# The common expert's up projection by pairs of tiles from the fifth tile on, with the ranks in another PSUM bank

## The chip, the cores and the metric

The kernel runs on one core of one Trainium2 chip. The metric is the device time of one execution in microseconds (us). All data are float32.

## What is computed

A vision block of one layer. 64 images of 3x96x96 are cut into 16x16 patches: 36 tokens an image, 2304 tokens of width 192. The steps are: a patch projection plus a position row; `h = h + attention(layernorm(h))` with 12 heads of 16; and `h = h + ffn(layernorm(h))`, where the FFN is a mixture of 9 experts, each 192 to 768 to 192 with an exact Gelu:

```
route_prob = softmax(xt @ Ws + bs);  p = max(route_prob);  routes = argmax(route_prob)
h = gelu(einsum('td,edf->tef', xt, W1) + b1, approximate=False)
out = einsum('tef,efd->ted', h, W2) + b2
common = out[:, 0, :];  sel = the row of out that routes picks
final = where(routes == 0, common * scaling, pe * sel + (1 - pe) * common)
```

Expert 0 (the common expert) is computed for every token, and the expert that the router picks for each token besides.

## The kernel before

**Tiles and steps.** The 2304 tokens are 18 tiles of 128. Everything up to the routing is one software pipeline, written out step by step: every engine runs its own `main_step(s, ...)` for s = 0 to 38, and an operation with lag L works in step s on tile s - L. On TensorE the lags that matter here are: projection of the attention output 10 (`project_o`), transpose of the normalised FFN input 11 (`transpose_xn2`), router 12 (`route`), up projection of the common expert 20 (`common_up` and `ffn_up_rest`), its down projection 21 (`common_down`). So tile 4 goes up in step 24 and down in step 25. The attention proper ends in step 23, `project_o` ends in step 27, `transpose_xn2` in step 28 and `route` in step 29. From step 30 on TensorE has only up and down projections.

**Order on TensorE within a step** of 24 or later: up projection, (in step 30: `count_ranks`), `route`, `common_down`, `transpose_xn2`, `project_o`.

**The up projection of one tile** is six chunks of 128 hidden columns. A chunk is a matmul of the 128x128 weights with a moving operand of 128 columns (L623, contraction over features 0 to 127) and a matmul with contraction over the last 64 features (L631). Chunks 0 to 2 of L631 use rows 0 to 63 of the array, chunks 3 to 5 rows 64 to 127, and the two kinds alternate. Chunks 0 to 2 lie in bank 6, 3 to 5 in bank 7. ScalarE applies Gelu with its bias chunk by chunk (L855). The down projection is six matmuls of 192 columns (L641) into bank 0 for even tiles and bank 2 for odd ones. In the trace a float32 matmul of these shapes shows as two records, so "x12" is six matmuls.

**What orders the steps.** All engines run their instructions in program order, with semaphores between them.
- `common_down(n)` for an even n waits until the router's sums of tile n + 10 are added (`log_copied`), since both use bank 0. For an odd n it doesn't.
- VectorE does in each step: `norm_xn2` (L915; it waits for GpSimd's `rstd_h2`, L1306 and L1308, of the step before), then `add_log` (L1043), then `add_common` (L1047), then `add_attention` (L1031, with L1034 and L1037), which waits for `project_o`.
- `project_o` in an odd step waits until `add_common` has emptied bank 0.
- `route(t)` waits for the saved transpose of tile t, which ScalarE copies (`copy_xn2`, L793 to L795) after its Gelus of the step before.
- `count_ranks` in step 30 (two matmuls of 162 columns, L703 and L704) counts, for each token, the earlier tokens of its expert. VectorE makes slots from it (`slots`, from L1153). GpSimd then scatters the 18 tiles of normalised rows by slot into a packed buffer in DRAM with 18 indirect DMAs (L1357). The sync engine waits for all 18 (`scattered`), loads the first two groups of 128 packed rows (L466), issues a load of slot rows and four stores of output rows (L467, L456), and goes on with the third group (L475).

**The second phase** is 25 groups of 128 packed rows, each with its own expert: transpose (L514, L515), copy by ScalarE, up (L623, L631), Gelu (L855), down (L641), scaled and added to the output. `W1R` holds the up weights of two groups.

**Memory.** One SBUF region, `ARENA`, holds first the patches and projection weights and later the hidden rows `HT`, the gathered rows and the routing scratch `RT`.

Of the kernel before, what the change touches and what calls it, by code (L numbers as in the profile page):

```python
# [22 lines left out]
ACT = mybir.ActivationFunctionType  # L23
AX = mybir.AxisListType

P = 128
# [4 lines left out]
TOKENS = IMAGES * SEQ  # L31
# [16 lines left out]
WCOLS = DFF + FH  # L48
EXPERTS = 9
EPS = 1e-5  # L50


GROUPS = (TOKENS + (EXPERTS - 1) * (P - 1)) // P
# [39 lines left out]
def vit_kernel(nc, patches, conv_w, conv_b, pos, w_qkv, w_o, gq, gk, w_router, w1, w1_rest, w2, b2, consts, ids, out):  # L93
# [4 lines left out]
    with ExitStack() as ctx:  # L98
# [36 lines left out]
            return CST[0:rows, a:b]  # L135


        ARENA = sb("ARENA", 5800)
        marks = [0]

        def cut(n):
            a = marks[0]
            marks[0] += n
            assert marks[0] <= 5800
            return ARENA[:, a:a + n]

        PT = [cut(KC * P) for _ in range(2)]
# [4 lines left out]
        QKN = [cut(4 * P) for _ in range(2)]  # L152
        VST = [cut(D) for _ in range(2)]
        marks[0] = 0
        HT = [cut(DFF) for _ in range(2)]
        XF = [cut(ROW) for _ in range(2)]
        YR = [cut(D) for _ in range(2)]
        BASE = [cut(D) for _ in range(4)]
# [52 lines left out]
        def xn2t(t):  # L211

            at = (2 + t % 2) * TOKENS + t // 2 * 2 * P
            return QK[:, at:at + 2 * P]

        def single(p):

# [272 lines left out]
        def _(pe):  # L490
# [154 lines left out]
            def common_down(n):  # L645
                if n >= 2:
                    pe.wait_ge(y_used, n - 1)
                if n % 2:
                    pe.wait_ge(qk_normed, TILES)
                else:  # L650
                    pe.wait_ge(log_copied, min(n + UP_START - MIXER_START, TILES))
                ffn_down(n, n % 2, 0)

            def route(t):
                s = t + 2 + MIXER_START
# [29 lines left out]
            def common_up(t):  # L685
# [3 lines left out]
                pe.wait_ge(xn2t_saved, t + 1)  # L689
                ffn_up_first(t, xn2t(t), W1, t >= 1)  # L690

            def turn_b1():
                pe.wait_ge(b1_in, 16)
                pe.wait_ge(h2_added, TILES - MIXER_START)
                pe.transpose(bank[0][:, 0:EXPERTS * FC], B1[0:EXPERTS * FC, :],
                             ident[0:EXPERTS * FC, 0:EXPERTS * FC]).then_inc(b1_turned, 1)

            def count_ranks():

                pe.wait_ge(chosen, 1)  # L700
                onehot = RT[:, 0:TE]
                pe.wait_ge(s_shifted, STEPS)
                pe.matmul(bank[4][:, 0:TE], const("before"), onehot, start=True, stop=True)  # L703
                pe.matmul(bank[5][:, 0:TE], const("ones"), onehot, start=True, stop=True).then_inc(ranks_done, 1)  # L704

            def main_step(s, ks):
                kc, kq, kp, kx, k_scores, k_weigh, kw, k1, kr, kf, kh = ks
                if s == TILES:
                    turn_b1()
                if kc is not None:  # L710
                    conv(kc, 0, KC // 2)
                if kf is not None:
                    common_up(kf)
                if k_scores is not None:
                    scores(k_scores, 0, k_scores)
                if kc is not None:
                    conv(kc, KC // 2, KC)
                if kf is not None:
                    ffn_up_rest(kf, xn2t(kf), W1)
                if s == MIXER_START + TILES + 2:  # L720
                    count_ranks()
                if kq is not None:
                    transpose_qk(0, kq)
                if k_weigh is not None:
                    weigh_v(k_weigh, 0)
                if kp is not None:
                    project_qk(kp)
                if kr is not None:
                    route(kr)
                if kh is not None:  # L730
                    common_down(kh)
                if k_scores is not None:
                    scores(k_scores, 1, k_scores)
                if k1 is not None:
                    transpose_xn2(k1)
                if kp is not None:
                    project_v(kp)
                if kw is not None:
                    project_o(0, kw)
                if kx is not None:  # L740
                    transpose_xn(0, kx)
                if k_weigh is not None:
                    weigh_v(k_weigh, 1)
# [34 lines left out]
        def _(act):  # L778
# [68 lines left out]
            def gelu(n, par, b1, guard):  # L847
                for g in range(2):
# [7 lines left out]
                                              bias=b1[:, bias:bias + 1])  # L856
                    last.then_inc(gelu_done, 1)

            def main_step(s, ks):
                kx, kv, kq, k_exp, k_o, ko, k1, kg = ks  # L860
                if s == TILES:
# [8 lines left out]
                    copy_qkT(kq)  # L870
                if k_exp is not None:
                    exp_scores(k_exp, 0, k_exp)
                if kg is not None:
                    gelu(kg, kg % 2, B1T, kg >= 2)
                if k_o is not None:
                    copy_o(k_o, 0)
                if k1 is not None:
# [34 lines left out]
        def _(dve):  # L912
# [237 lines left out]
            def slots():  # L1150

                dve.wait_ge(ranks_done, 1)
                then(dve.tensor_copy(by_expert(counts), bank[5][:, 0:TE].rearrange("p (t e) -> p e t", e=EXPERTS)))  # L1153
                then(dve.tensor_tensor_scan(running, const("keep"), counts, 0.0, ALU.mult, ALU.add))
                then(dve.tensor_tensor(before, running, counts, ALU.subtract))

# [5 lines left out]
                then(dve.tensor_tensor(per_e(2), per_e(1), per_e(0), ALU.subtract))  # L1162
                then(dve.tensor_scalar(per_e(3), per_e(2), float(P), None, ALU.mult))
                then(dve.tensor_tensor(by_expert(before), by_expert(before), per_e(3).unsqueeze(2).to_broadcast([P, EXPERTS, TILES]), ALU.add))
                then(dve.tensor_tensor(by_tile(scratch), bank[4][:, 0:TE].rearrange("p (t e) -> p t e", e=EXPERTS),
                                       before.rearrange("p (e t) -> p t e", t=TILES), ALU.add))
                then(dve.tensor_tensor(scratch, scratch, onehot, ALU.mult))
                then(dve.reduce_sum(top, by_tile(scratch), axis=AX.X))
# [284 lines left out]
```

## Time and profile before

| | |
|---|---|
| median of 3 runs | 388.1 us (388.03 to 388.18) |
| the profiled execution's own time | 386.88 us |
| its span | 385.0 us |
| TensorE busy | 364.3 us, 95% |
| VectorE, ScalarE, GpSimd busy | 172.2, 163.9, 188.3 us |
| granted TensorE clock, mean | 0.993 |

TensorE is busy nearly all of the span, and no other engine is half busy. The shares are means over phases that differ: the steps with attention, the steps without it, and the 25 groups. The views that count are those of single steps and of the passage to the groups. The profiled execution is 1.2 us below the median of the timed runs.

### The profile page before, as it was taken

To read this page: it belongs to the slowest core of one execution; us is meant where nothing else is said; L and a number is where in the kernel's file an instruction comes from. 1 tells how busy PE (TensorE), PEld (TensorE's weight loads), DVE (VectorE), ACT (ScalarE), POOL (GpSimd) and SP (SyncE) were. 2 spreads that over 40 slices of the span, in tenths; PEclk is the share of its full clock that TensorE was granted. 3 is DMA by queue.
4 is the path that set the end of the run, shared out by engine and by line. 5 is a ranking of instruction groups with operands and counts; after the bars stand their busy time and mean duration, and the time that the engine had idled before them with its cause. 6 is when DMAs were issued, how large, how long until landed. Compare 5 with 4: busy or idle time off the path is not lost. (4 is left out here: it accounts for less than half of the span.)

```text
span 385.0 us, 10445 instructions
## 1 busy us (share of the span) xinstructions
PE 364.3 (95%) x3291; PEld 325.6 (85%) x3292; DVE 172.2 (45%) x595; ACT 163.9 (43%) x553; POOL 188.3 (49%) x307
## 2 busy tenths in 40 slices
PE   6799999999999999899999999998999999999991
PEld 5677877788888888788888899997999999999991
DVE  3365767777777787544232265411112211111111
ACT  0122233333333354778444454335545544555540
POOL 1657977777777787443013006740333333444333
PEclk9999999999999999999999999999999999999997
DMA  7764335353321435435000905626666776676630
GB/s 243 234 207 120 101 105 162 94 156 91 90 79 48 130 113 166 124 97 187 20 0 14 245 2 142 217 80 147 150 170 160 176 187 164 167 165 164 155 76 0
DMA packets 40589, 49.58 MB, mean 129 GB/s; under 512 B 10412, under 2 KB 32313, under 8 KB 40553
## 3 DMA queue, kind: packets, MB, share of 16 engines
q1 hardware_dynamic: 34641, 42.95, 37.8%
q0 software_dynamic: 5024, 5.72, 8.8%
q10 hardware_dynamic: 888, 0.45, 0.4%
q8 instruction: 21, 0.34, 0.4%
q14 instruction: 15, 0.12, 0.1%
HBM read 39.84 MB, written 10.27 MB: 130 GB/s over the span
## 5 line engine op out<-in xcount | busy, mean ns | idle before, releaser
L641 PE MATMUL bank<-W,ARENA 128*128 (+1 forms) x516 | 94.6, 334 | 1.5 <-issue 1.2
L641 PEld LDWEIGHTS bank<-W,ARENA 128*128 128x128 f32 x516 | 82.8, 190 | 5.7 <-issue 1.5
L1371 POOL DMA_INDIRECT out<-ARENA,ID x25 | 39.4, 1575 | 71.3 <-DVE ARENA L1236 62.0
L855 ACT ACTIVATE ARENA<-score_banks,B1R 128x128 f32<-128x128 f32 x150 | 41.5, 376 | 39.8 <-PE score_banks L631 24.1
L855 ACT ACTIVATE ARENA<-score_banks,B1T 128x128 f32<-128x128 f32 x108 | 29.9, 375 | 31.8 <-PE score_banks L631 31.8
L1269 POOL TENSOR_TENSOR VS<-V,R 108x384 f32<-108x384 f32 x32 | 27.7, 865 | 30.5 <-DVE R L960 30.2
L1232 DVE TENSOR_TENSOR ARENA<-bank,B 128x192 f32<-128x192 f32 x25 | 8.9, 358 | 71.6 <-PE bank L641 71.6
L623 PE MATMUL score_banks<-RINGS,W1R 128*128 128x128 f32 x300 | 37.8, 276 | 1.4 <-ACT RINGS L795 0.8
L623 PEld LDWEIGHTS score_banks<-RINGS,W1R 128*128 128x128 f32 x300 | 35.6, 192 | 1.8 <-issue 1.8
L1260 POOL TENSOR_TENSOR RINGS<-QK,GM 128x216 f32<-128x216 f32 x64 | 34.1, 553 | 3.4 <-PE score_banks L579 3.4
L579 PEld LDWEIGHTS score_banks<-QK,RINGS 48*108 48x108 f32 x512 | 28.7, 171 | 6.1 <-issue 2.9
L579 PE MATMUL score_banks<-QK,RINGS 48*108 48x36 f32 x512 | 32.3, 262 | 0.0
L508 PE MATMUL bank<-ARENA 128*128 128x192 f32 x144 | 28.2, 336 | 2.3 <-DVE H L1009 1.3
L1357 POOL DMA_INDIRECT packed_tokens<-XN,SLOT x18 | 17.7, 985 | 23.3 <-issue 23.3
L816 ACT ACTIVATE QK<-bank 128x512 f32<-128x512 f32 x18 | 10.8, 598 | 41.1 <-PE bank L562 41.1
L623 PE MATMUL score_banks<-QK,W 128*128 128x128 f32 x216 | 27.5, 277 | 0.0
L623 PEld LDWEIGHTS score_banks<-QK,W 128*128 128x128 f32 x216 | 26.1, 191 | 0.2
L508 PEld LDWEIGHTS bank<-ARENA 128*128 128x128 f32 x144 | 22.9, 190 | 3.4 <-DMA ARENA<-in_patches 1.6
L596 PEld LDWEIGHTS bank<-RINGS,VS 108*64 108x64 f32 x512 | 17.6, 137 | 7.9 <-issue 6.0
L631 PE MATMUL score_banks<-RINGS,W1R 64*128 64x128 f32 x300 | 23.5, 289 | 0.0
L1367 POOL COPY ID<-SLOT_ROWS 128x1 int32 (+1 forms) x25 | 18.8, 752 | 9.3 <-DMA out<-ARENA 9.3
L596 PE MATMUL bank<-RINGS,VS 108*64 108x36 f32 x512 | 21.2, 228 | 1.9 <-ACT QK L809 1.4
(149 smaller groups left out, 622.1 us busy)
## 6 DMA issues: line engine op xcount, KB each, us to landing
W1R<-in_w SPq DMA_DIRECT2D x25, 384.0 KB
V<-v_rows SPq DMA_DIRECT2D x96, 54.0 KB
W<-in_w SPq DMA_DIRECT2D x9, 576.0 KB, 4.2
W1R<-in_w_rest SPq DMA_DIRECT2D x50, 96.0 KB
ARENA<-in_patches SPq DMA_DIRECT2D x11, 384.0 KB, 3.6
packed_tokens<-RINGS POOLq DMA_DIRECT2D x1, 2425.0 KB, 13.2
ARENA<-packed_tokens SPq DMA_DIRECT2D x25, 97.0 KB, 2.8
PT<-in_patches SPq DMA_DIRECT2D x6, 384.0 KB, 3.2
```

Source lines behind the costliest of these rows:

```text
L508: last = pe.matmul(bank[0][:, 0:D], PT[t % 3][:, c * P:c * P + P], CW[:, c * D:c * D + D], start=c == 0, stop=c == KC - 1)
L579: last = pe.matmul(score_bank(p, par)[0:K3, b * 512 + to:b * 512 + to + SEQ], KR[par][rows, m * K3:(m + 1) * K3], queries, start=True, sto ...
L596: last = pe.matmul(bank[3][b * DB:b * DB + DB, col:col + SEQ], VS[par][0:K3, at:at + DB], PR[par][0:K3, m * SEQ:(m + 1) * SEQ], start=True ...
L623: pe.matmul(bank[6 + g][:, at:at + P], w[:, c * P:c * P + P], x[:, 0:P], start=at == 0, stop=False, skip_group_check=True)
L631: last = pe.matmul(bank[6 + g][:, at:at + P], w[rows, DFF + at:DFF + at + P], x[rows, P:2 * P], start=False, stop=True, skip_group_check=True)
L641: last = pe.matmul(bank[2 * par][:, 0:D], HT[par][:, c * P:c * P + P], W2[:, bass.ds((expert * FC + c) * D, D)], start=c == 0, stop=c == F ...
L855: last = act.activation(HT[par][:, to:to + P], bank[6 + g][:, c * P:c * P + P], ACT.Gelu, bias=b1[:, bias:bias + 1])
L1260: last = pool.tensor_tensor(KR[par][:, c * nk // 2:(c + 1) * nk // 2].rearrange("p (n h k) -> p n h k", h=TRIPLE, k=SEQ), keys.unsqueeze(2 ...
L1269: pool.tensor_tensor(VS[par][0:K3, :].rearrange("p (m w) -> p m w", w=DB)[:, :, 0:TW].rearrange("p m (h d) -> p m h d", d=HD), V2[par][0:K ...
L1357: pool.indirect_dma_start(packed, bass.IndirectOffsetOnAxis(ap=SLOT[:, t:t + 1], axis=0), xn2_rows(t), None, bounds_check=GROUPS * P - 1, ...
L1367: pool.tensor_copy(ID[par][:, :], SLOT_ROWS[:, bass.ds(2 * n + 1, 1)].bitcast(I32)).then_inc(id_ready, 1)
L1371: pool.indirect_dma_start(out, bass.IndirectOffsetOnAxis(ap=ID[par][:, 0:1], axis=0), YR[par], None, bounds_check=TOKENS - 1, oob_is_err=F ...
```

## The change

Tiles 0 to 3 stay as they are (`ALONE = 4`). From tile 4 on, the up projection of tiles 2q and 2q + 1 is done together in the even step 20 + 2q. Six matmuls of 256 columns contract over the first 128 features and six over the last 64. The six results of 128x256 lie in four banks: 6, 7, 4 and 5 (4 and 5 are the score banks, free since step 22). Odd steps have no up projection. ScalarE applies six Gelus of 256 columns per pair, into a buffer for two tiles. The down projections stay one tile a step. The moving operand of the 256-column matmul is two blocks of 128 columns at a distance. `count_ranks` writes to bank 3 in place of banks 4 and 5, and waits for the last copy out of that bank instead of for the last scores. The arena grows from 5800 to 5912 columns.

```diff
+PAIR = 2
+ALONE = 4
+ARENA_COLS = 5912
...
-        HT = [cut(DFF) for _ in range(2)]
+        HTP = [cut(PAIR * DFF) for _ in range(2)]
+        HT = [HTP[1][:, i * DFF:(i + 1) * DFF] for i in range(2)]
...
+        def xn2t_pair(q):
+
+            both = QK[:, 2 * TOKENS:4 * TOKENS].rearrange("p (u n) -> p u n", u=PAIR)
+            return both[:, :, q * 2 * P:(q + 1) * 2 * P]
+
+        def pair_chunk(c):
+
+            b, at = ((bank[6], 0), (bank[6], 1), (bank[4], 0), (bank[7], 0), (bank[7], 1), (bank[5], 0))[c]
+            return b[:, at * PAIR * P:(at + 1) * PAIR * P]
...
-                ffn_down(n, n % 2, 0)
+                if n < ALONE:
+                    ffn_down(n, n % 2, 0)
+                    return
+                q, u = n // PAIR, n % PAIR
+                for c in range(FC):
+                    if c % (FC // 2) == 0:
+                        pe.wait_ge(gelu_done, 4 * q + 2 + 2 * (c // (FC // 2)))
+                    last = pe.matmul(bank[2 * u][:, 0:D], HTP[q % 2][:, (c * PAIR + u) * P:(c * PAIR + u + 1) * P],
+                                     W2[:, c * D:(c + 1) * D], start=c == 0, stop=c == FC - 1)
+                last.then_inc(y_done, 1)
...
+            def pair_up(q):
+
+                pe.wait_ge(gelu_done, 4 * q)
+                pe.wait_ge(s_shifted, STEPS)
+                pe.wait_ge(xn2t_saved, PAIR * q + 2)
+                for c in range(FC):
+                    pe.matmul(pair_chunk(c), W1[:, c * P:c * P + P], xn2t_pair(q)[:, :, 0:P],
+                              start=c % 3 != 1, stop=False, skip_group_check=True)
+
+            def pair_up_rest(q):
+
+                for c in range(FC // 2):
+                    at = DFF + c * P
+                    for g in range(2):
+                        rows = slice(g * DB, g * DB + DB)
+                        last = pe.matmul(pair_chunk(g * (FC // 2) + c), W1[rows, at:at + P], xn2t_pair(q)[rows, :, P:2 * P],
+                                         start=False, stop=True, skip_group_check=True)
+                        if c == FC // 2 - 1:
+                            last.then_inc(f1_done, PAIR)
...
-                pe.wait_ge(s_shifted, STEPS)
-                pe.matmul(bank[4][:, 0:TE], const("before"), onehot, start=True, stop=True)
-                pe.matmul(bank[5][:, 0:TE], const("ones"), onehot, start=True, stop=True).then_inc(ranks_done, 1)
+                pe.wait_ge(o_copied, STEPS)
+                pe.matmul(bank[3][:, 0:TE], const("before"), onehot, start=True, stop=True)
+                pe.matmul(bank[3][:, 2 * P:2 * P + TE], const("ones"), onehot, start=True, stop=True).then_inc(ranks_done, 1)
...
-                if kf is not None:
+                if kf is not None and kf < ALONE:
                     common_up(kf)
+                elif kf is not None and kf % PAIR == 0:
+                    pair_up(kf // PAIR)
...
-                if kf is not None:
+                if kf is not None and kf < ALONE:
                     ffn_up_rest(kf, xn2t(kf), W1)
+                elif kf is not None and kf % PAIR == 0:
+                    pair_up_rest(kf // PAIR)
...
+            def gelu_pair(q):
+
+                act.wait_ge(y_done, PAIR * q - 2)
+                for g in range(2):
+                    act.wait_ge(f1_done, 4 * q + 2 * g + 2)
+                    for c in range(g * (FC // 2), (g + 1) * (FC // 2)):
+                        last = act.activation(HTP[q % 2][:, c * PAIR * P:(c + 1) * PAIR * P], pair_chunk(c), ACT.Gelu,
+                                              bias=B1T[:, c:c + 1])
+                    last.then_inc(gelu_done, PAIR)
...
-                if kg is not None:
+                if kg is not None and kg < ALONE:
                     gelu(kg, kg % 2, B1T, kg >= 2)
+                elif kg is not None and kg % PAIR == 0:
+                    gelu_pair(kg // PAIR)
```

The two reads of the ranks in `slots` change to bank 3 in the same way.

## Rows read from the trace of the kernel before

**Rows 1.** The page: span, and busy time by engine.

```profile
span 385.0 us, 10445 instructions
...
PE 364.3 (95%) x3291; PEld 325.6 (85%) x3292; DVE 172.2 (45%) x595; ACT 163.9 (43%) x553; POOL 188.3 (49%) x307
```

**Rows 2.** Windows: each engine's busy us (instructions); then clock, DMA share, GB/s.

```profile
266.00:376.00 110.00, 110.00 (x913) 103.61 (x912) 20.19 (x71) 55.97 (x214) 40.87 (x46) 1.00 0.65 158
376.00:380.00 4.00, 1.13 (x7) 0.83 (x6) 0.76 (x3) 0.00 (x0) 2.21 (x3) 0.98 0.02 0
380.00:385.00 5.00, 0.00 (x0) 0.00 (x0) 0.00 (x0) 0.00 (x0) 1.14 (x1) 0.50 0.01 0
```

**Rows 3.** Timeline, the passage to the groups: start us, us, engine, line, operation [idle before].

```profile
255.18 0.97 POOL L1357 DMA_INDIRECT packed_tokens<-XN,SLOT  x1 [0.30 <-issue]
...
256.55 4.17 PE L641 MATMUL bank<-W,ARENA 128*128 128x192 f32 x24
...
257.73 0.82 SPq L466 DMA_DIRECT2D ARENA<-packed_tokens  x2
...
260.55 0.27 PE L514 MATMUL score_banks<-CST,ARENA 128*128 128x128 f32 x1
...
261.94 1.58 PE L623 MATMUL score_banks<-RINGS,W1R 128*128 128x128 f32 x12 [0.79 <-ACT RINGS L795]
...
262.35 0.45 SPq L475 DMA_DIRECT2D ARENA<-packed_tokens  x1
...
264.49 0.33 PE L514 MATMUL score_banks<-CST,ARENA 128*128 128x128 f32 x1
...
265.50 1.62 PE L623 MATMUL score_banks<-RINGS,W1R 128*128 128x128 f32 x12 [0.57 <-ACT ARENA L855]
```

**Rows 4.** Line 466, the loads of the first two groups.

```profile
DMA to landing us min/median/max: 2.0/2.0/2.0
```

**Rows 5.** Timeline, step 30: the ranks are read, the scatters start.

```profile
226.38 0.33 DVE L1153 COPY ARENA<-score_banks 128x162 f32<-128x162 f32 x1 [2.52 <-PE score_banks L704]
...
233.23 1.12 POOL L1357 DMA_INDIRECT packed_tokens<-XN,SLOT  x1 [18.09 <-issue]
```

**Rows 6.** Timeline, step 25, from its start to its down projection.

```profile
193.28 1.50 PE L623 MATMUL score_banks<-QK,W 128*128 128x128 f32 x12
193.48 0.36 DVE L1031 TENSOR_TENSOR H<-bank,H 128x192 f32<-128x192 f32 x1 [0.51 <-PE bank L615]
...
195.15 0.56 POOL L1308 TENSOR_TENSOR RSH<-VE,NEGHALF 128x1 f32<-128x1 f32 x1
...
195.74 0.38 DVE L915 TENSOR_SCALAR XN<-H,MVH,RSH 128x192 f32<-128x192 f32 x1 [1.07 <-POOL RSH L1308]
...
196.32 0.17 DVE L1043 TENSOR_TENSOR LOG<-bank,BR 128x9 f32<-128x9 f32 x1 [0.20 <-PE bank L667]
...
196.59 2.19 PE L641 MATMUL bank<-W,ARENA 128*128 128x192 f32 x12 [0.31 <-issue]
```

**Rows 7.** Timeline, step 29, from its start to its router matmuls.

```profile
217.89 1.50 PE L623 MATMUL score_banks<-QK,W 128*128 128x128 f32 x12
...
218.53 0.27 ACT L795 ACTIVATE QK<-bank 64x128 f32<-64x128 f32 x1
...
220.19 0.39 PE L666 MATMUL bank<-WR,QK 128*128 128x9 f32 x2
```

**Rows 8.** Timeline of TensorE, step 35: up projection, rest, down, next step's up.

```profile
245.54 1.50 PE L623 MATMUL score_banks<-QK,W 128*128 128x128 f32 x12
246.97 0.94 PE L631 MATMUL score_banks<-QK,W 64*128 64x128 f32 x12
247.84 2.22 PE L641 MATMUL bank<-W,ARENA 128*128 128x192 f32 x12
249.90 1.50 PE L623 MATMUL score_banks<-QK,W 128*128 128x128 f32 x12
```

**Rows 9.** Timeline of TensorE: the widest moving operand in the kernel, 384 columns.

```profile
147.11 0.81 PE L540 MATMUL bank<-ARENA,XT 65*128 65x384 f32 x2
147.75 0.29 PE L666 MATMUL bank<-WR,QK 128*128 128x9 f32 x2
```

**Rows 10.** Timeline: the six Gelus of one tile.

```profile
252.30 1.66 ACT L855 ACTIVATE ARENA<-score_banks,B1T 128x128 f32<-128x128 f32 x6 [2.69 <-PE score_banks L631]
```

More of the change, by code:

```diff
@@ L135, in const @@
             return CST[0:rows, a:b]
-        ARENA = sb("ARENA", 5800)
+        ARENA = sb("ARENA", ARENA_COLS)
         marks = [0]
@@ L143, in cut @@
             marks[0] += n
-            assert marks[0] <= 5800
+            assert marks[0] <= ARENA_COLS
             return ARENA[:, a:a + n]
@@ L1152, in slots @@
                 dve.wait_ge(ranks_done, 1)
-                then(dve.tensor_copy(by_expert(counts), bank[5][:, 0:TE].rearrange("p (t e) -> p e t", e=EXPERTS)))
+                then(dve.tensor_copy(by_expert(counts), bank[3][:, 2 * P:2 * P + TE].rearrange("p (t e) -> p e t", e=EXPERTS)))
                 then(dve.tensor_tensor_scan(running, const("keep"), counts, 0.0, ALU.mult, ALU.add))
@@ L1164, in slots @@
                 then(dve.tensor_tensor(by_expert(before), by_expert(before), per_e(3).unsqueeze(2).to_broadcast([P, EXPERTS, TILES]), ALU.add))
-                then(dve.tensor_tensor(by_tile(scratch), bank[4][:, 0:TE].rearrange("p (t e) -> p t e", e=EXPERTS),
+                then(dve.tensor_tensor(by_tile(scratch), bank[3][:, 0:TE].rearrange("p (t e) -> p t e", e=EXPERTS),
                                        before.rearrange("p (e t) -> p t e", t=TILES), ALU.add))
```

## The prediction

> **What bounds the kernel now.** I read the page first: TensorE is busy 364.3 of 385.0 us [rows 1]. That suggests that any TensorE time taken away shortens the kernel, so I looked next at where its work ends. The windows show the 25 groups as one solid block, 110.00 us busy in 110 us with the clock at 1.00 [rows 2]. The change does not touch this block. It can only move its start. So the question is what sets that start, and the timeline of the passage tells [rows 3]. Two things arrive almost together. TensorE ends its last two down projections and starts the first transpose at 260.55. The first two packed groups are loaded by DMAs issued at 257.73 that land 2.0 us later [rows 4], so at about 259.75 and 260.15. The second is followed back: the load waits for the last of 18 scatters, issued at 255.18 one behind the other, and the first of them starts at 233.23, 6.85 us after VectorE began on the ranks at 226.38 [rows 5]. VectorE had waited 2.52 us for TensorE's rank matmuls. So a chain of about 33.8 us leads from the rank matmuls (their end, about 226.3) to the landed groups, and apart from its start no TensorE instruction is in it. Its slack against TensorE's own work is only 0.5 us. **The end of the kernel follows the moment at which TensorE delivers the ranks in step 30.** Work saved behind the ranks is worth nothing; work put ahead of them costs in full.
>
> **Price of a pair.** One tile's up projection takes 245.54 to 247.84, 2.30 us: 1.43 for the six full matmuls (0.238 each) and 0.87 for the six of 64 rows, which run two at a time (0.29 for two) [rows 8]. At 192 columns six matmuls take 2.06, 0.343 each. The kernel has none of 256 columns, so I bound it. Below: the 384-column matmul takes 0.64 us [rows 9], or 1.667 ns a column, which gives 0.427. Above: the line through 128 and 192 columns gives 0.446. I take 0.437, so 2.62 for six. The last 64 features: two at a time cost at least 0.427, so 1.28 for three such; above, today's 0.29 plus the 0.213 of 128 more columns, 1.51; the far end is twice today's, 1.74. I take 1.38, near the lower ones, because at 128 columns two already take less than twice 0.213. **A pair costs 4.00 us (3.84 to 4.19; far end 4.42)**, against 4.60 for two tiles: 0.6 saved a pair, 4.2 over seven pairs.
>
> Where two matmuls on different rows of the array overlap, the rows give 0.29 us for two at 128 columns. The Trainium skill (TensorE: Matmul & The Clock Gate, Part 3, Measured speedup vs the span model) has the second cost only some 4 ns more. By that rule the pair would cost about 3.9, and the ranks 0.3 us less than below; the trace has a larger surplus at 128 columns, so I keep the bounds above.
>
> **What the change does to each step before the ranks.** The pair's work is not spread: an even step gets 4.00 where it had 2.30, an odd step gets nothing where it had 2.30. The even steps 24, 26, 28 and 30 have no waits on TensorE that the longer work could fill, so each becomes **1.70 longer, 6.80 in all**; in step 30 the ranks stand behind a pair that also holds tile 11, which was computed behind the ranks before.
>
> The odd steps can't give that back. In step 25 [rows 6] the up projection starts at 193.28 and the down projection at 196.59, because for an even tile it waits for the router's sums in bank 0. VectorE adds those after `norm_xn2`, which ends a chain that starts with the attention projection at the end of step 24: add at 193.48, statistics, GpSimd's power at 195.15, norm from 195.74 to 196.12, then the sums at 196.32. None of that is TensorE's up projection. It was the cover of this chain. Without it TensorE idles: the router matmuls run early (at about 193.95, once the sum of 193.48 and the copied transpose are there), the sums are added at 196.16 in place of 196.32, and the down projection starts **0.16 earlier**, not 2.30. The same holds for step 27: 0.32 together. Step 29 has no such chain, since no attention projection was made in step 28, but its router matmuls need the last transposed tile, and ScalarE ends that copy at 218.53 + 0.27 = 218.80 [rows 7]. They can start at about 219.0 in place of 220.19: **1.20 earlier**.
>
> Ranks: 6.80 - 0.32 - 1.20 = **5.28 us later** (4.64 with the cheapest pair, 6.04 with the upper, 6.96 with the far end). The change of the bank and of the awaited semaphore costs nothing: both semaphores are complete since step 23, and VectorE's two reads are of the same size. The cover of that is seven steps, so it can't be lost.
>
> **What lies behind the ranks.** TensorE's work there is nine down projections (18.5) and, in place of seven single tiles, three pairs (12.0): 30.5, to which I add up to 0.7 for a down projection that waits for VectorE while that waits for output stores. The groups land 33.4 us after the ranks. So TensorE, which was 0.5 us late for them, is now **about 3 us early and waits**. The 3 us are the savings of this part and are lost. The scatters, the first loads of group weights and the 16 output stores all hang on the ranks and move with them; none is passed by another queue's work that moves differently.
>
> The passage itself gains a little. The first transpose starts when the load lands instead of 0.6 later, and so does the first group. The third group's load stays where it is relative to the chain (262.35, lands about 264.4), since it stands behind four stores on SyncE's queue; TensorE waits for it as before, and the second group's start, which waited 0.57 for Gelus of the first, comes up to 0.64 earlier. I take **-0.5** (0 to -0.7). The groups then run as before, since each needs TensorE throughout.
>
> **ScalarE.** Six Gelus of 128 columns take 1.66 us [rows 10]; six of 256 take between that and 3.3. They start when the pair ends and must be done when `copy_xn2` is due, 2.9 us behind it (router 0.65, down 2.06, transpose 0.2). I expect 2.3, hidden. If they take 3.3, the cover fails by 0.4 in step 28 alone, the ranks come 0.4 later. The second half of the next down projection needs them at 3.1, which costs up to 0.3 a pair behind the ranks, where it is idle time anyway.
>
> **Sum.** 5.28 - 0.5 = 4.8 us. Against the profiled execution: 386.88 + 4.8 = 391.7. That execution is 1.2 below the median of the runs, so the median should go from 388.1 to **392.9 us**. A measurement of this kernel can tell about 0.2%, 0.8 us, from no change.
>
> **Rivals.**
> 1. *The clock falls.* The new idle times are the danger. Behind the last matmul of the kernel, at about 377.1, the granted clock falls from 1.00 (2.4 GHz) to 0.50 (1.2 GHz) by the end of the window 376 to 380, whose mean is 0.98 [rows 2]: so after about 2.7 us of idleness. New are about 3 us of idleness before the groups, and in steps 25 and 27 stretches of 3.15 us in which TensorE has only the small router matmuls. If it falls, one tile's down projection (2.06) or first group's up projection (2.3) takes twice its time: about 2.1 us for each fall, so 395.0 with one and 397.1 with two. Against it: no row shows a fall with work on both sides, and 2.7 us is close to the new gaps, not clearly below them. The Trainium skill (TensorE: Matmul & The Clock Gate, Why this matters for your kernels) warns against idle gaps between bursts of matmuls; the end of the trace agrees that idleness lowers the clock. I give 0.27.
> 2. *The odd steps close up* (this one ends on the other side). If the chain of rows 6 ran faster once VectorE and GpSimd have less to wait for, each of the three odd steps would give its 2.30 back. The ranks would move by 6.80 - 6.90 = -0.1, with the cheapest pair by -0.74, and the end by -0.6 to -1.2: 387.5 to 386.9. It decides from the point where the three steps together give back more than 6.3 of their 6.9. Rows 6 speak against it: the chain is anchored in the attention projection, and every link follows the one before within 0.4 us. 0.07.
> 3. *The load is not the bound.* If the groups could be there earlier relative to the ranks, TensorE's work would set the start: it would be 5.28 - 3.2 = 2 us later, 390.2. Rows 3 and 4 put the landing within 0.5 us of the use. 0.05.
> 4. *The pair saves nothing*, the change does not do what it says, for instance because the moving operand in two blocks is read slower: a pair costs 4.60. Ranks 4 x 2.30 - 1.52 = 7.7 later, the end at 395.3. The rows have no such operand. 0.06.
>
> **How the numbers follow.** Forecast (392.9, own range 391.5 to 394.9 from the prices of the pair and the passage) 0.52, rivals 0.27, 0.07, 0.05 and 0.06, and 0.03 for what I don't see. The range reaches from a little above rival 3 to about two falls of the clock: 391.0 to 396.8. It leaves out rivals 2 and 3 and the far tails. Slower: 0.52 + 0.27 + 0.05 + 0.06 + 0.02 = 0.92; rival 2 and the remainder fall half within 0.2%, half below: 0.04 and 0.04.
>
> **What would show it.** In the profile after: L623 with 128x256 operands at about 0.44 us start to start; in steps 25 and 27 TensorE idle ahead of L641, released by VectorE's L1043, about 3.1 us after L615; L1153 at about 231.7; the first L466 at about 263.0, with TensorE idle about 3 us before L514; then 110 us of groups as before. The prediction is wrong if L1153 comes before 230, if TensorE arrives at the groups with no idle time, or if the granted clock drops in a window around 198, 213 or 262.

## The result, and the profile after

The changed kernel is slower: median 398.99 us (396.47 to 409.05, 6 runs) against 388.14 us, ratio 1.0263, 95% interval 1.022 to 1.0306, so about 10 us. The prediction was 392.9 us with a range of 391.0 to 396.8: right in sign, but about 5 us too low, and the result lies outside the range. In some executions of either kernel the clock also stays low through steps 20 to 23, which the change does not touch; the ratio leaves those out, but the profiled execution of the changed kernel is one of them, so its times are read here as differences.

From step 24 to the ranks, the timeline of the changed kernel (L721 and L730 are the pair, L673 the down projection of the tiles from 4 on, L1102 the router's sums, L1212 the read of the ranks; columns as in [rows 3]):

```profile
200.86 2.86 PE L721 MATMUL score_banks<-QK,W 128*128 128x256 f32 x12
...
208.38 0.49 PE L629 MATMUL bank<-WO,OR 113*128 113x192 f32 x2
...
208.91 0.36 DVE L1090 TENSOR_TENSOR H<-bank,H 128x192 f32<-128x192 f32 x1 [0.51 <-PE bank L629]
...
211.17 0.38 DVE L974 TENSOR_SCALAR XN<-H,MVH,RSH 128x192 f32<-128x192 f32 x1 [1.07 <-POOL RSH L1367]
...
211.47 0.16 DVE L1102 TENSOR_TENSOR LOG<-bank,BR 128x9 f32<-128x9 f32 x1
...
211.73 2.19 PE L673 MATMUL bank<-W,ARENA 128*128 128x192 f32 x12 [1.70 <-issue]
...
246.94 0.33 DVE L1212 COPY ARENA<-bank 128x162 f32<-128x162 f32 x1 [4.40 <-PE bank L747]
...
250.95 2.75 PE L721 MATMUL score_banks<-QK,W 128*128 128x256 f32 x12
...
253.64 1.57 PE L730 MATMUL score_banks<-QK,W 64*128 64x256 f32 x12
...
253.78 1.12 POOL L1416 DMA_INDIRECT packed_tokens<-XN,SLOT  x1 [20.56 <-issue]
```

The odd step is as foretold: TensorE idles 1.70 us ahead of L673, and the sums of L1102 stand directly behind the norm of L974. From the start of step 24 to the read of the ranks it takes 46.08 us; before it took 226.38 - 187.31 = 39.07 [rows 5], the 187.31 being TensorE's first L623 of step 24. The distance from there to the first scatter is 6.84, before 6.85. The passage to the groups:

```profile
275.79 0.97 POOL L1416 DMA_INDIRECT packed_tokens<-XN,SLOT  x1 [0.30 <-issue]
...
278.17 0.82 SPq L480 DMA_DIRECT2D ARENA<-packed_tokens  x2
...
280.29 0.33 PE L528 MATMUL score_banks<-CST,ARENA 128*128 128x128 f32 x1 [2.67 <-DMA ARENA<-packed_tokens]
...
281.73 2.90 PE L637 MATMUL score_banks<-RINGS,W1R 128*128 128x128 f32 x12 [0.61 <-ACT RINGS L842]
```

TensorE waits 2.67 us for the packed rows, where it had no wait in [rows 3]. And the first group's six full matmuls take 2.90 in place of 1.58. That was not in the sum of the forecast; it is what rival 1 described. Windows of the same execution (columns as in [rows 2]) show why:

```profile
208.00:212.00 4.00, 1.85 (x12) 1.47 (x11) 1.71 (x6) 1.12 (x4) 0.77 (x2) 1.00 0.00 0
...
226.00:230.00 4.00, 3.89 (x15) 3.37 (x16) 0.36 (x1) 0.49 (x3) 1.74 (x1) 0.64 0.41 126
228.00:230.00 2.00, 1.89 (x7) 1.37 (x6) 0.36 (x1) 0.49 (x3) 0.00 (x0) 0.50 0.81 251
277.00:281.00 4.00, 1.33 (x8) 0.67 (x6) 0.18 (x2) 0.24 (x2) 0.00 (x0) 1.00 0.45 74
282.00:284.00 2.00, 2.00 (x10) 2.00 (x10) 0.69 (x2) 0.21 (x1) 0.00 (x0) 0.50 0.68 194
```

Behind the idle time of step 27 (window 228 to 230) and behind that of the passage (282 to 284) the granted clock is 0.50, 1.2 GHz in place of 2.4, while TensorE is busy 1.89 and 2.00 of 2 us. Around step 25 it stays at 1.00 (208 to 212), though TensorE idles there just as in step 27: the same idle time does not lower the clock every time.

### The profile page after: what moved, and what is told of

Same layout as the page of the kernel before. It is cut to its first block, busy times and chain, and to the rows that moved or that the text cites. A ratio compares the mean times of both kernels' runs of the same rounds, so it can differ in the third digit from the quotient of the medians.

```text
span 407.2 us, 10053 instructions
## 1 busy us (share of the span) xinstructions
PE 379.6 (93%) x3123; PEld 333.3 (82%) x3124; DVE 172.1 (42%) x595; ACT 156.7 (38%) x511; POOL 188.7 (46%) x307
## 4 chain that ended last, share of the span: by engine, by line
PE 74%; issue 5%; POOL 3%; DMA 3%; DVE 2%; SPq 2%; ACT 1%; POOLq 1%; DVEq 0%; ACTq 0%
PE bank L655 14%; PE score_banks L637 9%; PE score_banks L593 7%; PE bank L522 7%; PE score_banks L645 6%; PE bank L610 5%; PE bank L553 3%; POOL packed_tokens L1416 3%; PE bank L673 3%; PE score_banks L721 3%; PE bank L554 2%; PE bank L576 2%; PE bank L628 2%; DMA ARENA<-packed_tokens 2%; PE score_banks L730 1%
## 5 line engine op out<-in xcount | busy, mean ns | idle before, releaser
L655 PE MATMUL bank<-W,ARENA 128*128 (+1 forms) x348 | 67.4, 346 | 0.6 <-issue 0.3
L655 PEld LDWEIGHTS bank<-W,ARENA 128*128 128x128 f32 x348 | 58.9, 198 | 3.7 <-issue 0.4
L637 PE MATMUL score_banks<-RINGS,W1R 128*128 128x128 f32 x300 | 39.2, 282 | 0.8 <-ACT RINGS L842 0.6
L637 PEld LDWEIGHTS score_banks<-RINGS,W1R 128*128 128x128 f32 x300 | 36.8, 197 | 1.4 <-issue 1.4
L593 PEld LDWEIGHTS score_banks<-QK,RINGS 48*108 48x108 f32 x512 | 30.7, 182 | 6.5 <-issue 3.6
L593 PE MATMUL score_banks<-QK,RINGS 48*108 48x36 f32 x512 | 34.5, 272 | 0.0
L673 PE MATMUL bank<-W,ARENA 128*128 128x192 f32 x168 | 30.7, 338 | 3.7 <-issue 3.7
L673 PEld LDWEIGHTS bank<-W,ARENA 128*128 128x128 f32 x168 | 27.7, 194 | 5.3 <-issue 5.2
L912 ACT ACTIVATE ARENA<-score_banks,B1T 128x256 f32<-128x256 f32 x42 | 16.1, 482 | 30.1 <-PE score_banks L730 30.1
L610 PEld LDWEIGHTS bank<-RINGS,VS 108*64 108x64 f32 x512 | 19.2, 148 | 8.4 <-issue 6.3
L610 PE MATMUL bank<-RINGS,VS 108*64 108x36 f32 x512 | 22.8, 238 | 1.9 <-ACT QK L856 1.4
```

Source lines behind the costliest of these rows:

```text
L593: last = pe.matmul(score_bank(p, par)[0:K3, b * 512 + to:b * 512 + to + SEQ], KR[par][rows, m * K3:(m + 1) * K3], queries, start=True, sto ...
L610: last = pe.matmul(bank[3][b * DB:b * DB + DB, col:col + SEQ], VS[par][0:K3, at:at + DB], PR[par][0:K3, m * SEQ:(m + 1) * SEQ], start=True ...
L637: pe.matmul(bank[6 + g][:, at:at + P], w[:, c * P:c * P + P], x[:, 0:P], start=at == 0, stop=False, skip_group_check=True)
L655: last = pe.matmul(bank[2 * par][:, 0:D], HT[par][:, c * P:c * P + P], W2[:, bass.ds((expert * FC + c) * D, D)], start=c == 0, stop=c == F ...
L673: last = pe.matmul(bank[2 * u][:, 0:D], HTP[q % 2][:, (c * PAIR + u) * P:(c * PAIR + u + 1) * P], W2[:, c * D:(c + 1) * D], start=c == 0, ...
```

## The experiments

Two theories. **Theory 1:** the ranks come later by the structure alone (about 5.5 us at the end of the kernel), and on top of that the clock falls in the new idle times, about 2 us each. **Theory 2:** the structure alone costs 10 us. All ratios are against the kernel before on the same chip, with 95% intervals.

### Is it the clock? Useless matmuls in the idle times

The changed kernel once more, `a_again`.

> The changed kernel once more, as it is. Structure alone (ranks later by the measured pair of 4.18 us, so about 6.0, less 0.5 in the passage) gives 388.1 + 5.5 = 393.6. Theory 1, the clock falls in the new idle times and each fall costs about 2 us: 397 to 399, and the windows of 1 us show a clock below 1.00 behind idle time in step 25, 27 or 29 and at the first group, not everywhere. Theory 2, the structure costs more than was priced: 397 to 399 with a clock of 1.00 from step 24 to the end, and the ranks more than 7 us later than before.

Ratio 1.0267 (1.020 to 1.0334): the result again.

`b_busy_all`:

```diff
+            def keep_busy(n):
+                for _ in range(n):
+                    pe.matmul(bank[3][:, 0:D], W1[:, 0:P], W2[:, 0:D], start=True, stop=True)
...
+                if s == UP_START + ALONE + 1:
+                    pe.wait_ge(o_copied, STEPS)
+                    pe.wait_ge(v_copied, TILES)
+                if s == MIXER_START + TILES + 1:
+                    keep_busy(2)
                 if kr is not None:
                     route(kr)
+                if s in (UP_START + ALONE + 1, UP_START + ALONE + 3):
+                    keep_busy(4)
...
+            pe.wait_ge(slots_ready, 1)
+            keep_busy(7)
             for n in range(2):
                 transpose_group(0, n)
+            keep_busy(1)
```

> The changed kernel with matmuls of no use put into the idle times of TensorE: four of 192 columns ahead of the down projection in steps 25 and 27, two ahead of the router in step 29, seven ahead of the first group's transpose and one behind the second's. They write to a free bank and nobody waits for them. Theory 1 (clock): it becomes faster than the changed kernel by 3 to 5 us, to 393 to 395, though TensorE does more; clock 1.00 throughout. Theory 2 (structure): no gain, or up to 1 us slower.

Ratio 1.0112 (1.0071 to 1.0153). Doing more on TensorE takes some 6 us off, as theory 1 has it (and somewhat more than the 3 to 5 us expected) and theory 2 excludes.

`c_busy_end` has only the seven and one matmuls at the passage.

> Only the seven and the one useless matmuls at the passage to the groups. Theory 1: the fall at the first group is gone, 1 to 3 us faster than the changed kernel; falls in steps 25 to 29 remain. Theory 2: no difference.

`d_busy_odd` has only those of steps 25, 27 and 29.

> Only the useless matmuls in steps 25, 27 and 29. Theory 1: falls in those steps are gone, the one at the first group remains, 1 to 3 us faster than the changed kernel. Together the gains of this and of the one before should be about that of both at once. Theory 2: no difference.

1.0175 (1.0121 to 1.0229) and 1.0144 (1.011 to 1.0179): each keeps part of the gain, as theory 1 says. The sizes are not as expected: 3.4 and 4.6 us in place of 1 to 3 each, and their sum of 8 is more than the 6 of both at once. With intervals of about 2 us to either side these runs don't tell whether the gains add up. Beside a fall in step 20, taken up below, the profiled execution of the first shows clocks below 1.00 around 202 and 215 and none at the passage, that of the second only around 270, at the passage.

### The same with step 20 quiet

One more fall blurred these numbers: in step 20 TensorE idles 1.4 us ahead of its last attention matmuls, in the kernel before too, and sometimes the clock falls there. Four useless matmuls just there, in bank 2, remove it from all four of the following kernels:

```diff
+                if s == UP_START:
+                    pe.wait_ge(qk_normed, TILES)
+                    keep_busy(4, 2)
                 if k_weigh is not None:
                     weigh_v(k_weigh, 1)
```

`k20`, the kernel before with it:

> The kernel before with four useless matmuls of 192 columns in the idle time of 1.4 us of step 20, just ahead of the last attention matmuls, into a free bank. If idleness there makes the clock fall, no execution has the fall any more: all times at 386.4 to 387.4. If the cause is another, they spread over 386 to 400 as those of before.

Ratio 1.0014 (0.9984 to 1.0044), 387.5 to 391.1. No execution has the long fall, while six of the 25 of the kernel before beside it took 399.8 us or more; so the idle time is a condition of that fall. But all twelve lie above the 386.4 to 387.4 that I expected, and the lowest are 1 us above those of the kernel before. The span of its profiled execution is 1.1 us longer too, and 0.85 of that arises behind the second group, where TensorE waits 0.69 us for the packed rows of the fourth; the kernel before has no such wait. Why those rows come late is open.

`a20`, the changed kernel with it, and `b20`, the changed kernel with it and all of `b_busy_all`:

> The changed kernel with the same filling in step 20 and nowhere else. If idleness is the cause, only the new falls remain (steps 25, 27, 29 and the passage): 394 to 397, none near 405. If step 20 falls all the same, it spreads as the changed kernel.

> The changed kernel with the useless matmuls in step 20, in steps 25, 27 and 29 and at the passage. Every idle time over 1 us is filled, so this is the structure alone: ranks 5.7 us later than before, 0.5 gained in the passage, 391.5 to 392.5 in every execution. If falls remain in spite of it, the idle times are not what makes the clock fall.

a20: 396.66 us, ratio 1.0223 (1.0181 to 1.0264). b20: 392.16 us, ratio 1.0123 (1.0084 to 1.0162). Both spread more than expected: 394.8 to 398.7 for 394 to 397, and 391.1 to 393.4 for 391.5 to 392.5; the slowest of b20 has a mean clock of 0.989, the other five 0.994 or more. So the new falls cost 4.5 us, and the structure 3.8 us over k20 (388.37). The two profiled executions side by side, step 25 and the passage. First a20, its timeline:

```profile
196.54 0.39 PE L690 MATMUL bank<-WR,QK 64*128 64x9 f32 x2
...
198.64 4.18 PE L673 MATMUL bank<-W,ARENA 128*128 128x192 f32 x12 [1.71 <-issue]
202.61 0.42 PE L528 MATMUL bank<-CST,XN 128*128 128x128 f32 x1
...
236.54 0.33 DVE L1220 COPY ARENA<-bank 128x162 f32<-128x162 f32 x1 [4.40 <-PE bank L747]
...
267.88 0.82 SPq L480 DMA_DIRECT2D ARENA<-packed_tokens  x2
...
269.90 0.48 PE L528 MATMUL score_banks<-CST,ARENA 128*128 128x128 f32 x1 [2.68 <-DMA ARENA<-packed_tokens]
...
271.59 2.90 PE L637 MATMUL score_banks<-RINGS,W1R 128*128 128x128 f32 x12 [0.38 <-ACT RINGS L850]
...
277.18 1.62 PE L637 MATMUL score_banks<-RINGS,W1R 128*128 128x128 f32 x12 [0.59 <-ACT ARENA L910]
```

Its windows around them:

```profile
195.00:196.00 1.00, 0.77 (x6) 0.47 (x4) 0.48 (x2) 0.81 (x4) 0.00 (x0) 1.00 0.00 0
196.00:197.00 1.00, 0.70 (x4) 0.59 (x4) 0.71 (x3) 0.31 (x1) 0.00 (x0) 1.00 0.00 0
197.00:198.00 1.00, 0.00 (x0) 0.00 (x0) 0.00 (x1) 0.00 (x0) 0.73 (x2) 0.93 0.00 0
198.00:200.00 2.00, 1.36 (x4) 1.40 (x5) 0.46 (x2) 0.00 (x0) 0.04 (x1) 0.50 0.00 0
...
268.00:270.00 2.00, 0.10 (x1) 0.10 (x2) 0.00 (x0) 0.00 (x0) 0.00 (x0) 0.88 0.42 98
270.00:276.00 6.00, 5.62 (x28) 4.36 (x29) 1.10 (x3) 1.40 (x6) 0.18 (x1) 0.50 0.67 120
280.00:388.00 108.00, 108.00 (x892) 101.73 (x891) 20.05 (x70) 55.03 (x210) 40.92 (x46) 1.00 0.62 156
```

And b20, its timeline and two windows:

```profile
196.07 1.57 PE L752 MATMUL bank<-W 128*128 128x192 f32 x8
197.67 2.19 PE L673 MATMUL bank<-W,ARENA 128*128 128x192 f32 x12
...
231.54 0.33 DVE L1230 COPY ARENA<-bank 128x162 f32<-128x162 f32 x1 [4.40 <-PE bank L747]
...
262.82 0.82 SPq L480 DMA_DIRECT2D ARENA<-packed_tokens  x2
...
269.86 1.58 PE L637 MATMUL score_banks<-RINGS,W1R 128*128 128x128 f32 x12
```

```profile
197.00:198.00 1.00, 0.97 (x6) 0.70 (x6) 0.45 (x2) 0.00 (x0) 0.08 (x1) 1.00 0.00 0
198.00:200.00 2.00, 2.00 (x14) 1.79 (x12) 0.10 (x1) 0.00 (x0) 0.00 (x0) 1.00 0.00 0
```

The same six down matmuls (L673) take 4.18 us in a20 and 2.19 in b20. In a20 the clock falls within the microsecond 197 to 198, in which TensorE did nothing, behind one with the router matmuls only; the groups after 280 are as solid as before.

The account, in stretches. Step 24 (first L721 at 187.76 in a20, 186.80 in b20) to the read of the ranks: 39.07 before, 44.74 in b20, 48.78 in a20. So the structure puts **5.67** ahead of the ranks and the falls **4.04**. Ranks to the first load: 31.35, 31.28 and 31.34, unchanged. First load to the second group's first matmul: 7.77 before, 7.04 in b20 (-0.73) and 9.30 in a20 (+1.53, a fall worth 2.26). From the shared state of step 24 on that makes +4.9 for b20 and +11.2 for a20.

### Is it the distribution of the pair's work?

`f_split`:

```diff
-                elif kf is not None and kf % PAIR == 0:
+                elif kf == ALONE:
                     pair_up(kf // PAIR)
+                elif kf is not None and kf % PAIR and kf + 1 < TILES:
+                    pair_up((kf + 1) // PAIR)
```

> The changed kernel with the pair's work laid over two steps: its six full matmuls of 256 columns in the odd step before, its 64-row matmuls in the even step (the pair of tiles 4 and 5 stays whole in step 24). By my theory what costs is the distribution, not the pair: odd steps have their cover back (2.69 where 2.30 stood), even steps get 1.49 where 2.30 stood, the ranks come at about the time of before (step 24 +1.9, the others together -1.8). 0.5 us is gained in the passage to the groups: 387.6 if the clock holds, up to 390 if it falls at the passage, where TensorE still idles some 2.4 us. If the pairs themselves cost time (bank contention, the strided operand), it stays above 392.

Ratio 1.0046 (1.001 to 1.0081), where the changed kernel has 1.0263: 8 of the 10 us are gone with the same matmuls in the same banks. The new split takes away the lost time and the falls in the odd steps together. The profiled execution reads the ranks at 226.63 against 226.38. Its first load goes out 32.93 us behind that, 1.58 more than before, since it comes 4.15 us behind the start of the last scatter in place of 2.55; TensorE waits 2.17 us for it, and the clock falls.

`g_split_ranks` moves the ranks of step 30 ahead of the up projection as well:

```diff
                 if s == TILES:
                     turn_b1()
+                if s == MIXER_START + TILES + 2:
+                    count_ranks()
...
-                if s == MIXER_START + TILES + 2:
-                    count_ranks()
                 if kq is not None:
```

> As the one before, and the rank matmuls of step 30 stand ahead of the up projection instead of behind it. If the end follows the ranks, it moves with them by the 1.5 us of the 64-row matmuls: 386.1 if the clock holds, with about 1.3 us of idle time left before the groups. If the end does not follow the ranks, it is equal to the one before.

0.998 (0.9941 to 1.0018), about 2.5 us under f_split, where I expected 1.5. The end does follow the ranks. The surplus goes with the passage, where the profiled execution has no wait for the load and no fall of the clock (I had expected 1.3 us of idle time there), and its load goes out 31.35 us behind the read of the ranks, as before. How much of the 2.5 us is the late load of f_split and its fall is not shown.

`i_logfirst` is the changed kernel with VectorE's order turned from step 25 on:

```diff
+                if kl is not None and s > UP_START + ALONE:
+                    add_log(kl)
                 if k1 is not None:
                     norm_xn2(k1)
...
-                if kl is not None:
+                if kl is not None and s <= UP_START + ALONE:
                     add_log(kl)
```

> The changed kernel, but from step 25 on VectorE adds the router's sums (L1043 of before) ahead of the norm of the FFN input instead of behind it. My theory is that the down projection of steps 25 and 27 stands behind the chain projection, statistics, power, norm only because VectorE does the sums last. Then it starts about 1.8 us instead of 3.1 behind the step's start: the ranks come 2.6 us earlier than in the changed kernel, and with two idle times halved there are fewer falls of the clock: 391 to 394. If something else held the odd steps back (the transposed tile, bank 0), nothing changes: 396 to 399.

Ratio 1.007 (1.0034 to 1.0105), nearly three quarters of the loss gone. From the start of step 24 to the read of the ranks it takes 41.95 us, 2.8 less than in b20 (2.6 expected), and no 2 us window of steps 24 to 30 has a clock below 0.97. In step 25 the wait ahead of L673 falls from 1.70 to 0.31:

```profile
207.65 0.36 DVE L1090 TENSOR_TENSOR H<-bank,H 128x192 f32<-128x192 f32 x1 [0.52 <-PE bank L629]
...
208.81 0.17 DVE L1102 TENSOR_TENSOR LOG<-bank,BR 128x9 f32<-128x9 f32 x1
...
209.08 2.19 PE L673 MATMUL bank<-W,ARENA 128*128 128x192 f32 x12 [0.31 <-issue]
209.91 0.38 DVE L974 TENSOR_SCALAR XN<-H,MVH,RSH 128x192 f32<-128x192 f32 x1 [0.94 <-POOL RSH L1369]
```

The order of two instructions on VectorE, one of them of 0.17 us, held TensorE back.

`e_alone12`:

```diff
-ALONE = 4
+ALONE = 12
```

> Pairs only from tile 12 on, that is only behind the ranks. Steps up to 31 are those of before, so the ranks come as before. TensorE saves 3 x 0.4 us behind them and arrives at the groups 0.4 us before they land: end 0 to 0.5 us earlier than before, 387.6 to 388.1, no new idle time over 1 us, so no new fall of the clock. If pairs cost in themselves, 1 us or more slower than before.

1.0053 (1.0017 to 1.0089): not what I expected. The ranks are read at 226.39, as before, and the first load goes out at 257.68, so pairs behind the ranks delay nothing ahead of the groups. But in the profiled execution TensorE arrives early, waits 0.55 and 0.49 us at the first group and then 1.88 us for the third, whose load took 1.70 us to issue in place of 0.45, and the clock is low from 266 to 270 (mean 0.57). The pairs save 1.3 us behind the ranks; a late load and the fall behind it take more than that. Whether the load is late in the other executions too is not shown.

### Parts that should cost nothing, and a misplaced filling

`k_busy21` put the four matmuls of k20 into step 21, one step behind the idle time; the three kernels below it carry them too:

```diff
+                if s == UP_START + 1:
+                    keep_busy(4, 2)
                 if k_weigh is not None:
                     weigh_v(k_weigh, 1)
```

> The kernel before, with four useless matmuls of 192 columns in the one idle time of 1.4 us of step 21, into a free bank. In several executions, of the kernel before too, the clock fell there. If idleness there is the cause, this kernel has no execution with a fall in steps 21 to 23, and its times lie together at 386.6 to 387.2, under the median of before. If the fall has another cause, its times spread as those of before.

Ratio 1.0084 (1.0048 to 1.0119). It did not test its question. It shows that useless matmuls in a step without idle time cost: step 21 takes 11.26 us in place of 9.95. The profiled execution also waits 1.45 us for the packed rows of the fourth group, as k20 does.

`k_bank3_21`: of the change only the lines of `count_ranks` and `slots` that put the ranks in bank 3 and wait for `o_copied`.

> As the one before, and of the change only the ranks in bank 3 with their other semaphore. I expect the same time within 0.2 us. If the bank or the wait cost anything, it shows here as a later first scatter.

1.0091 (1.0052 to 1.013), equal to k_busy21 within the intervals: this part costs nothing that can be measured.

`h_ranks_21`: the two moved lines of g_split_ranks in the kernel before.

> The kernel before with the same filling in step 21, and the ranks ahead of the up projection in step 30: they come 2.3 us earlier, nothing else is changed. By my account TensorE's own work then sets the start of the groups, which in the kernel before stands only 0.5 us behind the landing: gain 0 to 0.5 us. If the groups waited for the landing alone, the gain would be 2.3 us.

1.0074 (1.0033 to 1.0115) against 1.0084: a gain of 0.4 us that the intervals do not separate from none. In the profiled executions the ranks are read 2.08 us earlier (224.93 for 227.01) and the first load goes out 1.73 earlier, but the first group's transpose starts at 261.50 in place of 261.19, without a wait. In the kernel before, TensorE's own work is the other bound of the passage.

`m_all`: split, ranks first, sums ahead of the norm, five matmuls at the passage, and the misplaced filling.

> The version the experiments point to: pairs laid over two steps, ranks first in step 30, router's sums ahead of the norm, and TensorE kept busy in step 21 and at the passage (five matmuls, and one behind the transposes). Ranks about 1.5 us earlier than before, TensorE at the groups before they land, clock 1.00 from step 21 on: 385.0 to 386.0 in every execution, faster than before by 0.2% or more. If useless matmuls don't hold the clock, it spreads over 386 to 399 as its relatives.

1.0065 (1.0038 to 1.0091), a miss: the filling was in the wrong step, so a fall at 158 to 174 was still there in the profiled execution, and the other executions pay for the filling, which alone costs k_busy21 0.8%.

### The version that beats both

`g20` is g_split_ranks with the filling in step 20.

> Pairs laid over two steps, ranks first in step 30, and the filling in step 20. Without a fall this version showed 385.8 to 386.3. I expect 385.5 to 386.5 in every execution, 1.0 us or more under the median of before. If it gains only by chance of the clock, it is equal to the first of these four.

386.55 us, ratio 0.9976 (0.9953 to 0.9999) to the kernel before; 385.9 to 388.1 over twelve executions, six of them above the 386.5 that I expected at most. The gain of 0.9 us is small, and the interval ends just below 1. It is 1.8 us under k20 and 10.1 under a20. Three rows of its timeline and one of its windows:

```profile
219.27 2.75 PE L721 MATMUL score_banks<-QK,W 128*128 128x256 f32 x12
...
224.80 0.51 PE L746 MATMUL bank<-ARENA,CST 128*128 128x162 f32 x2
...
225.51 1.57 PE L730 MATMUL score_banks<-QK,W 64*128 64x256 f32 x12
```

```profile
266.00:376.00 110.00, 110.00 (x912) 103.73 (x912) 20.23 (x71) 55.89 (x214) 40.92 (x46) 1.00 0.63 158
```

The pair's full matmuls stand in the odd step, the ranks between the two halves, and the block of the groups is that of [rows 2]. The ranks are read at 225.61, 0.77 earlier than before, and the first load goes out 0.77 earlier too, but the first transpose only 0.08: TensorE's own work is the bound here. The lowest executions, 385.9, lie 0.5 us below the lowest of the kernel before (386.4).

## Why the prediction was right in part, and where it failed

- **What bounds the kernel: right.** The end follows the ranks; from their read to the first load it took 31.3 us in all three kernels compared (32.93 in f_split, where the load came late), and moving work behind them or ahead of them moved the end (f_split, g_split_ranks). This holds for ranks that come later than before; earlier ones gain next to nothing (h_ranks_21), as the slack of 0.5 us said.
- **Price of a pair: at the upper bound.** I took 4.00 and the trace has 4.18 (250.95 to 253.64 to 255.13): 2.69 for the full matmuls, 1.49 for the 64-row ones. The upper bounds (0.446 a full matmul, which is 0.448 when the line is worked out again, and 0.50 for two of 64 rows) were the true values: the surplus over 1.667 ns a column that 128 and 192 columns show stays at 256. The Trainium skill (TensorE: Matmul & The Clock Gate, Part 3, Measured speedup vs the span model) has the second of two overlapping matmuls add some 4 ns, by which a couple would take, as an estimate, about 0.43; the trace, with 0.50, does not agree.
- **Even and odd steps: right.** Steps 24 and 25 together grew by 1.59 in b20 (186.80 to 201.13, before 187.31 to 200.05), 26 and 27 the same, 28 and 29 by 0.60, the up projection of step 30 by 1.88. With 1.88 for each even step the odd ones gave back 0.29, 0.29 and 1.28, where I had 0.16, 0.16 and 1.20. i_logfirst shows that the sums behind the norm are the cause. Sum 5.67, forecast 5.28.
- **The passage: right** without a fall, -0.73 against -0.5 (my bound was -0.7), and the wait of 2.7 against about 3.
- **The step that failed** is the clock: the sum 5.28 - 0.5 = 4.8 has no term for a fall, and rival 1 got a chance of only 0.27. The falls are the normal case: every execution of a20 has a mean clock of 0.986 or less, and together they cost 4.5 us, more than the structure with its 3.8. So the main case of the prediction was wrong, and rival 1 described what happened. Its price of one fall was about right (I had 2.1; a20 shows 2.64 and 1.40 in steps 24 to 27, 2.26 at the passage), and so was its time with two falls, 397.1. But the range ended at 396.8, just short of that, and the profiled execution of a20 has three falls: step 25, step 27 and the passage. They came where the prediction itself said that it would be wrong.
- **What misled me** was the one fall that the trace before shows, 2.7 us behind the last matmul. I took this as a length that a gap must reach. The windows of a20 show a fall about 1 us after the router matmuls, and no gap between two records there is longer than 1.71 us; in the whole stretch of some 3 us between `project_o` and L673 TensorE had nothing but those four records. The Trainium skill (TensorE: Matmul & The Clock Gate, Why this matters for your kernels) advises against idle gaps between bursts of matmuls, and a20 and b20 agree with it.
- 5.67 - 0.73 and 4.04 + 2.26 make 11.2 for the profiled execution of a20, the longest of its six; the medians give 3.8 + 4.5 = 8.3. The changed kernel without the filling in step 20 is 10 us slower; what makes up the rest between 8.3 and 10 is not shown.

## What to carry to other kernels

Before making one engine's work cheaper, ask what its old length covered: here TensorE's up projection hid a chain of VectorE and GpSimd in every step, so merging two steps' work into one saved 0.4 us and cost 1.6. Larger matmuls can still pay if their pieces are laid where the cover was, and if what others wait for (the ranks) is put ahead of them. New idle time on TensorE must be priced twice, once as time and once as a clock that may halve for the work behind it; here that second price was 1.4 to 2.6 us for each fall.

## What the runs showed of the hardware that was not expected

- The granted clock fell from 1.00 to 0.50 in stretches of about 3 us where TensorE was not fully idle but had only four records of 9-column matmuls, and useless matmuls in those stretches kept it at 1.00 in the profiled execution and made the kernel 4.5 us faster (a20 to b20). The same stretch in step 25 of the changed kernel left the clock at 1.00.
- Once fallen, the clock can stay low under full load. In the profiled execution of the changed kernel the windows of steps 20 to 23 read:

```profile
162.00:188.00 26.00, 25.74 (x175) 23.15 (x174) 6.72 (x23) 10.39 (x25) 5.56 (x9) 0.50 0.17 45
```

  25.74 us busy of 26, and 0.50 throughout; behind the falls of a20 it came back within about 6 us of work. What tells the two cases apart is not settled.
- A float32 matmul of 256 columns costs 0.448 us behind another one (2.69 for six); two of 64 rows that run beside each other cost 0.50.
